# A Mamba-like block with an FFN on one core: the first step gets an order of its own, GpSimd splits W_in, TensorE transposes the identity while it waits, and the bias is prepared in two operations

## The chip, the cores and the metric

The kernel runs on one core of a Trainium2 chip. Its time is the device time of one execution in microseconds (us). Five engines take part, each with an instruction queue of its own, worked off in order: TensorE (PE), VectorE (DVE), ScalarE (ACT), GpSimd (POOL) and SyncE (SP), which here only issues transfers. They meet at semaphores alone: `then_inc` counts one up when an instruction is done, `wait_ge` holds a queue until it has reached a number.

## The reference, cut to what matters

```python
xn = layernorm(x)                                   # x: 4 x 1024 x 256
x_inner, z = split(xn @ W_in.T)                     # 512 channels each
xc = silu(causal_conv4(x_inner) + conv_b)
h[t] = 0.95 * h[t-1] + xc[t]                        # a scan over 1024 tokens
s_C = (xc @ W_x.T)[:, 16:]
y = (h * (s_C @ exp(B_log).T) * silu(z)) @ W_out.T
attn = layernorm(xn + y) * ln_g + ln_b
ffn = mx_quantise(xn) @ mx_quantise(W).T + bias     # blocks of 32, FP6 grid
out = x + attn + ffn
```

## The kernel before

A batch element is 1024 tokens. Per element the kernel holds the 512 channels as four chunks `c` of 128 partitions by 1024 tokens, and the tokens as two halves `g` of 512 (four tiles of 128). Every product in which precision matters is done as three fp32r matmuls on a high and a low part (`split_product`), so every operand is split first: ACT copies it to fp32r (`xn_high`, `y_high`, `w_in_high`), and DVE or POOL subtracts that from the original (`xn_low`, `y_low`, `w_in_low`).

The elements are pipelined by hand. `step(s)` of each engine lists, in the order of its queue, the work of three elements: `prev`, `here` and `nxt`. Functions wrapped in `of_batch` do nothing for an element that doesn't exist. `every_step` runs s = -1, 0, 1, 2, then `last_step` follows. Step -1 is thus only the front half of element 0 (`nxt`), with the preparation of the weights put between by `if first(nxt)`:

- DVE: token statistics, `scale_ffn_weight` and `round_ffn_weight` (L1208 to L1223, operations of 128x512 in SBUF), `w_in_low(0)`, `xn_low` of both halves, `dequantise_ffn_weight`, `block_max`, `w_in_low(1)`, the two middle taps of the convolution of chunks 0 and 1 (`conv_tap2`, `conv_tap1`, L1110), then `w_ffn_low`, `sum_w_out` and `scan` of chunk 0 (L1139).
- POOL: `rstd_1`, `prepare_b`, `prepare_bias`, `conv_tap0` of chunks 0 and 1 (L412), then `gate` of chunk 0 (L420).
- ACT: `normalise`, `w_in_high(0)`, `xn_high`, `w_in_high(1)`, `b_exponential`, `mask_b`, then `taps` of chunks 0 and 1, `silu_x(0)`.
- PE: `t_norm` of both halves (transposes of xn), `x_half` 0 to 2, `w_ffn_transposes` after `x_half(1)`, and `z_half`, `x_half(3)` and `s_product` when their PSUM slots come free.

`prepare_bias` makes two rows, high and low part of ln_b + ffn_b, for one matmul with ones; each of its seven POOL operations but the last waits in `chain` for its own end. It also scales g_row by 16, since `inverse_deviation` works on the sum of squares and not on the mean.

PSUM has three slots of two banks, which hold a chunk each, and two banks for the output. Which chunk lies in which slot stands in fixed lists, and `slot_free` makes PE wait for the last reader of what a slot held:

```python
SLOT_X = [1, 2, 0, 2]
SLOT_Z = [1, 1, 1, 2]
SLOT_TN = [0, 1]
SLOT_CB = [0, 1, 2, 0]
```

The loads of SP's queue are x of element 0 in two halves, W_in in two halves of columns (`w_in_f`, in the buffer rs), W_out, x of element 1, and, once that has landed, x of element 2. The small weights and the rows are loaded from ACT's queue.

## Time and profile before

| | |
|---|---|
| median of 3 runs | 264.28 us (263.95 to 264.28) |
| the profiled execution | 264.83 us, of it 263.0 us span from the first to the last instruction |
| DVE busy | 228.6 us, 87% of the span |
| PE busy | 216.9 us, 82% |
| POOL busy | 200.9 us, 76% |
| ACT busy | 154.6 us, 59% |
| mean granted clock of TensorE | 0.959 |

Busy time counts an instruction from its start to its end, and so holds the time in which one was started and stood still. The shares are of the whole span; the step that is changed takes about its first 35 us. In the rows below L12 is line 12 of the kernel, `out<-in` are tiles by name, and `<-` in brackets names what ended the idle time before.

### The profile page before, as it was taken

How to read it: one execution, taken by the hardware profiler on the slowest of the kernel's cores; microseconds unless marked ns; L12 is line 12 of the kernel's file. 1: busy time of each engine (PE TensorE's matmuls, PEld its weight loads, DVE VectorE, ACT ScalarE, POOL GpSimd, SP SyncE). 2: the span in 40 equal slices, each digit the busy share in tenths (PEclk: the TensorE clock that was granted, in tenths of full speed). 3: DMA queues.
4: the chain of work that ended last, by engine and by line, in shares of the span. 5: the costliest groups of instructions: out<-in, count | busy, mean ns of one | idle time of the engine just before them, and what ended most of it. 6: DMA issues, size and time to landing. Idle time of an engine off the chain costs nothing.

```text
span 263.0 us, 3473 instructions
## 1 busy us (share of the span) xinstructions
PE 216.9 (82%) x1252; PEld 180.8 (69%) x1252; DVE 228.6 (87%) x311; ACT 154.6 (59%) x234; POOL 200.9 (76%) x130
## 2 busy tenths in 40 slices
PE   0369974878899999879999969879999992977991
PEld 0348843357689886668898928767988951867991
DVE  3899999997799899958999999588999997594875
ACT  2796591455956537667995347728976364454320
POOL 1427949999997779999689599979498999933423
PEclk9999999797999999999999999979999998697999
DMA  7965000000000000004112000000202000002032
GB/s 230 262 217 159 1 2 0 0 1 0 0 2 0 1 2 0 0 2 150 40 53 80 0 0 1 2 0 0 82 0 80 4 0 0 0 2 80 26 137 80
DMA packets 10809, 11.18 MB, mean 42 GB/s; under 512 B 680, under 2 KB 10152, under 8 KB 10792
## 3 DMA queue, kind: packets, MB, share of 16 engines
q1 hardware_dynamic: 9520, 9.96, 11.8%
q10 hardware_dynamic: 1272, 0.99, 1.4%
q8 instruction: 10, 0.16, 0.3%
q14 instruction: 7, 0.06, 0.1%
HBM read 6.76 MB, written 4.19 MB: 42 GB/s over the span
## 4 chain that ended last, share of the span: by engine, by line
DVE 33%; POOL 27%; PE 16%; issue 10%; ACT 10%; DMA 4%; POOLq 0%; ACTq 0%; DVEq 0%
POOL hy L420 9%; POOL rstd L400 6%; DVE hy L1139 6%; POOL xc L412 6%; DVE xc L1110 6%; DVE fx L1177 3%; DVE rs L1167 2%; DMA y<-fx 2%; ACT xn L625 2%; DVE fx L1169 2%; DVE bn L1047 2%; DVE y_lo L1157 2%; DVE xq L1093 2%; ACT rs L718 2%; ACT y_hi L694 2%
## 5 line engine op out<-in xcount | busy, mean ns | idle before, releaser
L807 PE MATMUL slot<-xn_hi,w_in_lo 128*128 128x512 f32 x128 | 53.2, 416 | 6.1 <-DVE xn_lo L1099 2.6
L412 POOL TENSOR_TENSOR xc<-xc,tap 128x1021 f32<-128x1021 f32 x16 | 46.1, 2883 | 13.9 <-DVE xc L1110 13.9
L808 PE MATMUL slot<-xn_lo,w_in_hi 128*128 128x512 f32 x128 | 51.6, 403 | 0.0
L809 PE MATMUL slot<-xn_hi,w_in_hi 128*128 128x512 f32 x128 | 51.4, 402 | 0.0
L1139 DVE TENSOR_TENSOR_SCAN hy<-decay,xc 128x1024 f32<-128x1024 f32 x16 | 46.5, 2909 | 0.1
L420 POOL TENSOR_TENSOR hy<-hy,sz 128x1024 f32<-128x1024 f32 x14 | 43.4, 3098 | 2.3 <-ACT sz L672 2.3
L1110 DVE SCALAR_TENSOR_TENSOR xc<-slot,cw,xc 128x1023 f32<-128x1023 f32 (+1 forms) x32 | 40.2, 1265 | 2.1 <-ACT tap L662 1.6
L807 PEld LDWEIGHTS slot<-xn_hi,w_in_lo 128*128 128x128 f32 x128 | 24.7, 193 | 17.6 <-issue 3.9
L677 ACT ACTIVATE xc<-xc 128x1024 f32<-128x1024 f32 x16 | 17.0, 1060 | 29.0 <-POOL xc L412 29.0
L809 PEld LDWEIGHTS slot<-xn_hi,w_in_hi 128*128 128x128 f32 x128 | 24.7, 193 | 6.1
L808 PEld LDWEIGHTS slot<-xn_lo,w_in_hi 128*128 128x128 f32 x128 | 24.8, 193 | 4.9
L658 ACT ACTIVATE xc<-slot,cb,cw 128x1024 f32<-128x1024 f32 x16 | 19.2, 1201 | 12.7 <-PE slot L809 12.7
L625 ACT ACTIVATE xn<-x_in,nmr,rstd 128x256 f32<-128x256 f32 x32 | 16.6, 590 | 13.5 <-POOL nmr L404 13.3
L906 PE MATMUL obank<-w_out_hi,y_hi 128*128 128x256 f32 x96 | 24.3, 285 | 0.0
L905 PE MATMUL obank<-w_out_lo,y_hi 128*128 128x256 f32 x96 | 24.3, 285 | 0.0
L430 POOL TENSOR_TENSOR y_lo<-hy,y_hi 128x1024 fp32r<-128x1024 f32 x9 | 22.4, 2525 | 2.5 <-ACT y_hi L694 2.4
L803 PE MATMUL slot<-ident,xn 128*128 128x128 f32 x64 | 11.2, 332 | 14.5 <-ACT xn L625 11.7
L1152 DVE TENSOR_TENSOR hy<-slot,hy 128x1024 f32<-128x1024 f32 x16 | 18.9, 1210 | 3.3 <-PE slot L873 3.2
L400 POOL TENSOR_TENSOR rstd<-ve,minus_half 128x4 f32<-128x4 f32 x8 | 17.1, 2134 | 5.6 <-DVE ve L1063 5.6
L803 PEld LDWEIGHTS slot<-ident,xn 128*128 128x128 f32 x64 | 9.1, 172 | 16.4 <-issue 12.2
L872 PE MATMUL slot<-s_lo,b_t 128*128 128x512 f32 x32 | 14.7, 458 | 6.2 <-DVE s_lo L1145 5.9
L672 ACT ACTIVATE sz<-slot 128x1024 f32<-128x1024 f32 x14 | 14.3, 1024 | 7.7 <-POOL hy L420 7.4
(125 smaller groups left out, 586.3 us busy)
## 6 DMA issues: line engine op xcount, KB each, us to landing
x_in<-L_attn_x SPq DMA_DIRECT2D x3, 1024.0 KB, 5.4
y<-fx SPq DMA_DIRECT2D x6, 512.0 KB, 3.0
x_in<-L_attn_x SPq DMA_DIRECT2D x2, 512.0 KB, 4.1
rs<-L_attn_W_in SPq DMA_DIRECT2D x2, 512.0 KB, 10.0
y<-x_in SPq DMA_DIRECT2D x3, 256.0 KB, 2.1
fx<-L_attn_W_out SPq DMA_DIRECT2D x1, 512.0 KB, 12.9
fx<-L_ffn_weight ACTq DMA_DIRECT2D x1, 256.0 KB, 5.3
xc<-L_attn_B_log ACTq DMA_DIRECT2D x1, 256.0 KB
```

Of the source, the lines that this page charges most:

```text
L400: pool.tensor_tensor(rstd1[:, b % XS, cols], ve1[:, cols], minus_half[:, cols], ALU.pow).then_inc(rstd1_ready, 1)
L412: pool.tensor_tensor(xc[:, c, TAPS - 1:], xc[:, c, TAPS - 1:], tap0[:, c % 2, 0:n], ALU.add).then_inc(conv_ready, 1)
L420: pool.tensor_tensor(hy[:, c, :], hy[:, c, :], sz_of(b, c), ALU.mult).then_inc(hsz_ready, 1)
L430: pool.tensor_tensor(y_lo_of(b, c), hy[:, c, :], y_hi_of(b, c).bitcast(F32), ALU.subtract).then_inc(ylo_pool, 1)
L625: act.activation(xn[:, t, :], x_in[:, b % XS, t, :], ACT.Identity, bias=nmr1[:, b % XS, t:t + 1], scale=rstd1[:, b % XS, t:t + 1]).then_in ...
L807: pe.matmul(dst, w_lo, m_hi, start=first, stop=False)
L808: pe.matmul(dst, w_hi, m_lo, start=False, stop=False)
L809: return pe.matmul(dst, w_hi, m_hi, start=False, stop=last)
L905: pe.matmul(bank[:, 0:DM], y_hi[:, c, tok], w_out_lo[:, c, :], start=c == 0, stop=False)
L906: pe.matmul(bank[:, 0:DM], y_hi[:, c, tok], w_out_hi[:, c, :], start=False, stop=False)
L1110: dve.scalar_tensor_tensor(xc[:, c, back:], slot[SLOT_X[c]][:, 0:SEQ - back], cw[:, c, k:k + 1], xc[:, c, back:], ALU.mult, ALU.add).then_ ...
L1139: dve.tensor_tensor_scan(hy[:, c, :], decay[:, 0:1].broadcast_to([P, SEQ]), xc[:, c, :], 0.0, ALU.mult, ALU.add).then_inc(scan_done, 1)
```

## The change

- Step -1 becomes a function `first_step` of each engine, and `every_step` starts at 0. In it DVE does `block_max` right behind each `xn_low`; PE does `w_ffn_transposes` after `x_half(2)`; ACT does `b_exponential` and `mask_b` right behind `xn_high`, ahead of `taps`.
- Element 0 has PSUM slots of its own for x, z and the cb products, and the waits of PE follow them. `x_half(0)` waits for `xn_lo` half by half.
- `w_in_high` (ACT) and `w_in_low` (DVE) go; POOL does both in `split_w_in`, ahead of `prepare_b`.
- PE does 48 transposes of the identity ahead of `t_norm`, and 12 more ahead of `x_half(0)`.
- ln_b and ffn_b are loaded into two partitions each of a tile that POOL clears first; `prepare_bias` is one copy, and a subtraction over 64 partitions. The factor 16 of g_row goes, since `inverse_deviation` now divides by DM.
- SP waits for W_in before it issues the load of W_out.

```diff
+        FIRST_SLOT_X = [2, 0, 1, 0]
+        FIRST_SLOT_Z = [2, 1, 2, 1]
+        FIRST_SLOT_CB = [0, 2, 1, 0]
+        def slot_x(b, c):
+            return slot[(FIRST_SLOT_X if first(b) else SLOT_X)[c]]
...
-            for s in range(-1, LAST):
+            for s in range(LAST):
                 step(s)
...
+            sp.wait_ge(w_in_loaded[1], 16)
             sp.dma_start(w_out_f, w_out.rearrange("(c p) o -> p c o", p=P)).then_inc(w_out_loaded, 16)
...
+            pool.memset(bias_f, 0.0).then_inc(bias_cleared, 1)
             pool.memset(decay[:, :], DECAY).then_inc(const_ready, 1)
...
-                pool.tensor_scalar(ve2[:, cols], ssq[:, cols], DM * LN_EPS, None, ALU.add).then_inc(ve2_ready, 1)
+                pool.tensor_scalar(ve2[:, cols], ssq[:, cols], 1.0 / DM, LN_EPS, ALU.mult, ALU.add).then_inc(ve2_ready, 1)
...
+            def split_w_in(h):
+                cols = slice(h * DI, (h + 1) * DI)
+                pool.wait_ge(w_in_loaded[h], 16)
+                pool.tensor_copy(w_in_hi[:, :, cols], w_in_f[:, :, cols]).then_inc(w_in_hi_ready, 1)
+                pool.wait_ge(w_in_hi_ready, h + 1)
+                pool.tensor_tensor(w_in_lo[:, :, cols], w_in_f[:, :, cols], w_in_hi[:, :, cols].bitcast(F32),
+                                   ALU.subtract).then_inc(w_in_lo_ready, 1)
...
-                for i in range(3):
-                    pool.wait_ge(row_loaded[i], 16)
-                chain(pool.tensor_scalar(g_row[:, :], g_row[:, :], math.sqrt(DM), None, ALU.mult))
-                chain(pool.tensor_tensor(bias_a, bias_a, bias_b, ALU.add))
-                chain(pool.tensor_copy(bias_hi[:, :], bias_a))
-                chain(pool.tensor_tensor(bias_b, bias_a, bias_hi[:, :].bitcast(F32), ALU.subtract))
-                chain(pool.tensor_scalar(bias_b, bias_b, ident[:, 1:2], None, ALU.mult))
-                chain(pool.tensor_scalar(bias_a, bias_hi[:, :].bitcast(F32), ident[:, 0:1], None, ALU.mult))
-                pool.tensor_tensor(bias_rows[:, :], bias_a, bias_b, ALU.add).then_inc(bias_ready, 1)
+                pool.wait_ge(row_loaded[1], 16)
+                pool.wait_ge(row_loaded[2], 16)
+                chain(pool.tensor_copy(bias_rows[:, :], bias_f))
+                low = slice(P // 2, P)
+                pool.tensor_tensor(bias_rows[low, :], bias_f[low, :], bias_rows[low, :].bitcast(F32), ALU.subtract).then_inc(bias_ready, 1)
+                pool.wait_ge(bias_ready, 1)
+
+            def first_step(nxt):                       # POOL
+                rstd_1(nxt, 0)
+                rstd_1(nxt, 1)
+                split_w_in(0)
+                split_w_in(1)
+                prepare_b()
+                prepare_bias()
+                conv_tap0(nxt, 0)
+                conv_tap0(nxt, 1)
+                gate(nxt, 0)
...
-            for i, (dst, src) in enumerate(((g_row[:, :], ln_g), (bias_a, ln_b), (bias_b, ffn_b))):
-                act.dma_start(dst, src.rearrange("(a d) -> a d", a=1).broadcast_to([P, DM])).then_inc(row_loaded[i], 16)
+            act.dma_start(g_row[:, :], ln_g.rearrange("(a d) -> a d", a=1).broadcast_to([P, DM])).then_inc(row_loaded[0], 16)
+            act.wait_ge(bias_cleared, 1)
+            for i, src in enumerate((ln_b, ffn_b)):
+                act.dma_start(bias_f[i * P // 4:P:P // 2, :],
+                              src.rearrange("(a d) -> a d", a=1).broadcast_to([2, DM])).then_inc(row_loaded[1 + i], 16)
+
+            def first_step(nxt):                       # ACT
+                normalise(nxt, 0)
+                normalise(nxt, 1)
+                xn_high(nxt, 0)
+                xn_high(nxt, 1)
+                b_exponential()
+                mask_b()
+                taps(nxt, 0)
+                w_x_twice()
+                taps(nxt, 1)
+                w_ffn_high()
+                silu_x(nxt, 0)
+                taps(nxt, 2)
...
                 for g in range(2):
+                    if e0 == 0:
+                        pe.wait_ge(xn_lo_ready, 2 * b + g + 1)
...
+            def warm_up(n):
+                for i in range(n):
+                    transpose(obank[0][:, 0:P], ident[:, :])
+
+            def first_step(nxt):                       # PE
+                pe.wait_ge(ident_ready, 2)
+                warm_up(48)
+                t_norm(nxt, 0)
+                t_norm(nxt, 1)
+                warm_up(12)
+                x_half(nxt, 0)
+                x_half(nxt, 1)
+                x_half(nxt, 2)
+                w_ffn_transposes()
+                pe.wait_ge(tap1_done, 1)
+                z_half(nxt, 0)
+                pe.wait_ge(tap1_done, 2)
+                x_half(nxt, 3)
+                pe.wait_ge(tap1_done, 3)
+                z_half(nxt, 1)
+                pe.wait_ge(sz_ready, 1)
+                z_half(nxt, 2)
+                s_product(nxt)
+                pe.wait_ge(sz_ready, 2)
+                z_half(nxt, 3)
...
-                slot_free(nxt, (y_ready, NCH * here + 2, here))
+                slot_free(nxt, (y_ready, NCH * here + (3 if first(here) else 2), here))
                 t_norm(nxt, 1)
...
+            def first_step(nxt):                       # DVE
+                for g in range(2):
+                    token_stats(nxt, g)
+                    aggregate(nxt, g)
+                    mean_var(nxt, g)
+                scale_ffn_weight()
+                round_ffn_weight()
+                xn_low(nxt, 0)
+                block_max(nxt, 0)
+                xn_low(nxt, 1)
+                block_max(nxt, 1)
+                block_scale(nxt, 0)
+                dequantise_ffn_weight()
+                conv_tap2(nxt, 0)
+                conv_tap1(nxt, 0)
+                block_inverse(nxt, 0)
+                block_scale(nxt, 1)
+                conv_tap2(nxt, 1)
+                conv_tap1(nxt, 1)
+                w_ffn_low()
+                sum_w_out()
+                block_inverse(nxt, 1)
+                scan(nxt, 0)
```

## Rows read from the trace of the kernel before

**Rows 1.** The page: the span, and the chain that ended last, by engine.

```profile
span 263.0 us, 3473 instructions
...
DVE 33%; POOL 27%; PE 16%; issue 10%; ACT 10%; DMA 4%; POOLq 0%; ACTq 0%; DVEq 0%
```

**Rows 2.** Timeline of DVE, 9 to 36 us: start, duration (us), instruction, count, idle before.

```profile
10.26 0.43 DVE L1218 CAST hy<-fx 128x512 fp8e4<-128x512 f32 x1
10.72 0.69 DVE L1221 TENSOR_TENSOR fx<-hy,fx 128x512 f32<-128x512 fp8e4 x1
...
11.91 0.43 DVE L1223 TENSOR_SCALAR hy<-hy 128x512 f32<-128x512 f32 x1
13.45 1.22 DVE L1205 TENSOR_TENSOR w_in_lo<-rs,w_in_hi 128x1024 fp32r<-128x1024 f32 x1 [1.11 <-ACT w_in_hi L588]
14.60 2.35 DVE L1099 TENSOR_TENSOR xn_lo<-slot,xn_hi 128x1024 fp32r<-128x1024 f32 x2
...
18.30 1.66 DVE L1228 SCALAR_TENSOR_TENSOR fx<-fx,hy 128x512 f32<-128x512 f32 x1
...
24.98 2.60 DVE L1110 SCALAR_TENSOR_TENSOR xc<-slot,cw,xc 128x1023 f32<-128x1023 f32 x2 [0.30 <-ACT tap L662]
...
32.52 2.97 DVE L1139 TENSOR_TENSOR_SCAN hy<-decay,xc 128x1024 f32<-128x1024 f32 x1
35.41 0.72 DVE L1047 BATCH_NORM_STATS2 bn<-x_in 128x6 f32<-128x256 f32 x2
```

**Rows 3.** Timeline of POOL, first 34 us.

```profile
9.59 0.69 POOL L404 TENSOR_TENSOR nmr<-nm,rstd 128x4 f32<-128x4 f32 x1
...
17.75 1.67 POOL L484 TENSOR_TENSOR xc<-xc,b_t 128x512 f32<-128x512 f32 x1 [7.46 <-ACT b_t L594]
...
20.92 1.28 POOL L488 TENSOR_TENSOR b_t<-xc 128x512 fp32r<-128x512 f32 x1 [1.51 <-ACT xc L602]
...
29.40 3.94 POOL L412 TENSOR_TENSOR xc<-xc,tap 128x1021 f32<-128x1021 f32 x2
```

**Rows 4.** Timeline of ACT, 22 to 43 us.

```profile
22.62 1.21 ACT L658 ACTIVATE xc<-slot,cb,cw 128x1024 f32<-128x1024 f32 x1 [1.78 <-PE slot L809]
...
41.54 1.06 ACT L677 ACTIVATE xc<-xc 128x1024 f32<-128x1024 f32 x1 [1.87 <-POOL xc L412]
```

**Rows 5.** Timelines of DVE and POOL in the next steps: two pairs that overlap.

```profile
42.00 6.22 DVE L1139 TENSOR_TENSOR_SCAN hy<-decay,xc 128x1024 f32<-128x1024 f32 x2
...
71.22 0.70 DVE L1080 TENSOR_SCALAR s<-amax 128x32 f32<-128x32 f32 x1
...
42.02 4.05 POOL L412 TENSOR_TENSOR xc<-xc,tap 128x1021 f32<-128x1021 f32 x1 [0.51 <-DVE xc L1110]
...
71.85 5.75 POOL L430 TENSOR_TENSOR y_lo<-hy,y_hi 128x1024 fp32r<-128x1024 f32 x2
```

**Rows 6.** Groups of POOL by line and shape, 0 to 80 us: count, busy us, mean ns.

```profile
L500 POOL TENSOR_TENSOR w_out_lo<-fx,w_out_hi 128x1024 fp32r<-128x1024 f32 x1 | 2.4, 2384 | 0.0
...
L512 POOL CAST bias_hi<-hy 128x256 fp32r<-128x256 f32 x1 | 0.4, 397 | 0.1
...
L506 POOL CAST ones_r<-xc 128x128 fp32r<-128x128 f32 x1 | 0.3, 289 | 0.1
```

**Rows 7.** Busy time by stretch: length, PE, PEld, DVE, ACT, POOL, clock, DMA, GB/s.

```profile
17.00:22.60 5.60, 5.55 (x13) 4.43 (x14) 5.50 (x6) 3.46 (x6) 3.28 (x4) 1.00 0.45 137
...
63.00:63.50 0.50, 0.50 (x5) 0.50 (x4) 0.00 (x0) 0.50 (x1) 0.42 (x2) 0.50 0.00 0
64.00:64.50 0.50, 0.50 (x5) 0.41 (x4) 0.50 (x1) 0.00 (x0) 0.50 (x1) 1.00 0.00 0
```

**Rows 8.** Timeline of PE, 58 to 65 us: transposes.

```profile
60.64 1.94 PE L803 MATMUL slot<-ident,xn 128*128 128x128 f32 x8 [1.08 <-ACT xn L625]
```

**Rows 9.** The tile rs, into which W_in is loaded: issues and landings.

```profile
L353 SPq DMA_DIRECT2D rs<-L_attn_W_in x2: 469/484/500, 1.8 to 2.3; - x2
...
DMA to landing us min/median/max: 8.9/10.0/11.2
```

More of the change, by code:

```diff
@@ L293, in build, with slot_z, slot_cb @@
         SLOT_CB = [0, 1, 2, 0]
+        FIRST_SLOT_CB = [0, 2, 1, 0]
+        def slot_x(b, c):
+            return slot[(FIRST_SLOT_X if first(b) else SLOT_X)[c]]
+        def slot_z(b, c):
+            return slot[(FIRST_SLOT_Z if first(b) else SLOT_Z)[c]]
+        def slot_cb(b, c):
+            return slot[(FIRST_SLOT_CB if first(b) else SLOT_CB)[c]]
         def half(g):
@@ L468, in scale_g @@
                 wait(pool, norm_ready, NT * b + HT * (g + 1))
+                if first(b) and g == 0:
+                    pool.wait_ge(row_loaded[0], 16)
                 pool.tensor_tensor(rs[:, cols, :], rs[:, cols, :],
@@ L532, in step @@
                 dequantise(here, 1)
-                if first(nxt):
-                    prepare_b()
-                    prepare_bias()
                 y_low(here, 0)
@@ L671, in silu_z @@
                     wait(act, hsz_ready, NCH * b + c)
[L672 removed]
+                act.activation(sz_of(b, c), slot_z(b, c)[:, :], ACT.Silu).then_inc(sz_ready, 1)
             @of_batch
@@ L734, in step @@
                 normalise(nxt, 1)
-                if first(nxt):
-                    w_in_high(0)
                 norm_2(prev, 0)
@@ L839, in x_half @@
             def x_half(b, c):
-                if c == 0:
-                    wait(pe, xn_lo_ready, 2 * (b + 1))
-                    if first(b):
-                        pe.wait_ge(w_in_lo_ready, 1)
-                in_projection(SLOT_X[c], c * P, x_ready)
+                if c == 0 and first(b):
+                    pe.wait_ge(w_in_lo_ready, 1)
+                in_projection(b, slot_x(b, c), c * P, x_ready)
             @of_batch
@@ L871, in cb_product @@
                 for g in range(2):
-                    pe.matmul(slot[SLOT_CB[c]][:, half(g)], b_t[:, c * P:(c + 1) * P], s_lo[:, half(g)], start=True, stop=False)
-                    mm = pe.matmul(slot[SLOT_CB[c]][:, half(g)], b_t[:, c * P:(c + 1) * P], s_hi[:, half(g)],
+                    pe.matmul(slot_cb(b, c)[:, half(g)], b_t[:, c * P:(c + 1) * P], s_lo[:, half(g)], start=True, stop=False)
+                    mm = pe.matmul(slot_cb(b, c)[:, half(g)], b_t[:, c * P:(c + 1) * P], s_hi[:, half(g)],
                                    start=False, stop=True)
@@ L976, in step @@
                 x_half(nxt, 1)
-                if first(nxt):
-                    w_ffn_transposes()
                 slot_free(nxt, (xd_lo_ready, 2 * here + 2, here), (xn_lo_ready, 2 * nxt + 1, nxt))
@@ L1268, in step @@
                 y_product(here, 2)
-                if first(nxt):
-                    scale_ffn_weight()
-                    round_ffn_weight()
-                    w_in_low(0)
                 xn_low(nxt, 0)
@@ L1276, in step @@
                 xn_low(nxt, 1)
-                if first(nxt):
-                    dequantise_ffn_weight()
                 block_max(nxt, 0)
@@ L1288, in step @@
                 block_inverse(nxt, 0)
-                if first(nxt):
-                    w_in_low(1)
                 conv_tap2(nxt, 0)
@@ L1296, in step @@
                 conv_tap1(nxt, 1)
-                if first(nxt):
-                    w_ffn_low()
-                    sum_w_out()
                 block_inverse(nxt, 1)
```

41 lines of the change are left out of this document (12 added, 29 removed).

## The prediction

> **What bounds the kernel now.** I read the page first, then the timelines of the first 60 us, engine by engine. By the chain of work that ended last, no single engine sets the end: DVE has 33% of it and POOL 27% [rows 1]. So what the changed step gives is read at one place, the end of DVE's first scan, behind which DVE and POOL run without a break into step 0. It is started at 32.52 and DVE's next instruction comes at 35.41 [rows 2]. A scan needs only 2.1 us (below), so it really began at 33.3. That is the end of POOL's two `conv_tap0`, 29.40 + 3.94 [rows 3]. Three queues arrive there together: DVE, in order, at 32.5; POOL, late because `prepare_b` and `prepare_bias` hold it until 29.4; ACT and PE, which give `taps(0)` at 22.62, when `x_half(0)` is done [rows 4].
>
> **A resource that both DVE and POOL need.** At 42.0 us DVE has two scans in 6.22 us, and POOL started a `conv_tap0` at 42.02 that took 4.05, where two at 29.40 took 3.94 together, 1.97 each [rows 3, 5]. One after the other fits: scan 2.1, tap 2.0, scan 2.1, sum 6.2. And the instruction that waited goes ahead of a successor of the one that ran. The same holds for a plain TENSOR_SCALAR: DVE's of 128x32 at 71.22 took 0.70, while one of 128x512 takes 0.43, and it ended at 71.92, just after the POOL operation before the one of 71.85 had ended [rows 2, 5]. In the changed step itself: L1228 took 1.66, where L1221 of the same width took 0.69, while POOL's L484 ran to 19.42, and that took 1.67 against 1.28 for L488 [rows 2, 3]. So DVE's instructions that work from SBUF alone and POOL's exclude each other for a whole instruction. `xn_low` is not among these: it reads PSUM and keeps its 1.2 us [rows 2].
>
> The Trainium skill (SBUF — State Buffer, Who interferes with whom) says the same: an exclusive lock, held for a whole instruction, against DVE instructions with two SBUF inputs or in a two-port mode, while `tensor_reduce` and those with one SBUF input are free. The durations above agree. By a plain reading of the change without this rule, the sum would be that of the first rival.
>
> **The change, part by part.**
>
> *GpSimd splits W_in.* It takes 1.22 us twice and 1.11 us of idle from DVE [rows 2], and two copies from ACT, and puts four operations on POOL. The subtractions are like L500: 2.38 us each. The copies have no row at 128x1024: by the casts, 0.289 us at 128 columns and 0.397 at 256, it is 0.108 per 128, so 0.397 + 6 x 0.108 = 1.05 us [rows 6]. The lower bound is 1.0; the upper one is that of a two-input operation, 2.38 [rows 6]. I take 1.05, the same operation being nearest. All four: 6.9 us.
>
> When do they start? POOL is free at 10.28 [rows 3]; the first half of W_in lands at 1.8 + 8.9 = 10.7 [rows 9], perhaps a little earlier since W_out no longer shares the queue. There DVE is in `round_ffn_weight`: L1218 until 10.69, L1221 from 10.72 [rows 2]. Two orders are possible.
>
> Order A, the copy comes first: copy 10.7 to 11.7, L1221 to 12.4, subtraction to 14.8, L1222 to 15.2, second copy to 16.3, L1223 to 16.7, second subtraction to 19.1. DVE's rounding ends at 16.7, not 12.3, and `xn_low(0)` begins at 16.7 instead of 14.60 [rows 2]: 2.1 later.
>
> Order B, L1221 comes first: L1221 to 11.4, copy to 12.5, L1222 to 12.9, subtraction to 15.3, L1223 to 15.7, then the second pair to 19.2. `xn_low(0)` begins at 15.7.
>
> *DVE's queue from there.* Before, it was 24.98 - 14.60 = 10.4 us from `xn_low(0)` to `conv_tap2(0)` [rows 2]. Of this go `w_in_low(1)` 1.2, idle 0.30, and the 1.0 that L1228 stood still; a reciprocal of 0.3 moves behind. That leaves 7.6. POOL's `prepare_b` is later now: its first operation 19.15 to 20.4 (1.28) meets only `xn_low` and `block_max`; the mask on ACT takes 1.5 as before (from 19.42 to 20.92) [rows 3]; its second, from 21.9, and the two casts of 0.29 and 0.40 fall among the four operations of `dequantise_ffn_weight`, each before one of them: 1.28 + 0.29 + 0.40 = 2.0. In order A `conv_tap2(0)` begins at 16.7 + 7.6 + 2.0 = 26.3, in order B at 25.2 (some 0.1 less standing still), against 24.98. From it to the scan were 7.54 us [rows 2]; the order within is the same. The scan begins at 33.8 in A and 32.7 in B, and now at once, since POOL, with the short bias, ends `conv_tap0(1)` by then. It ends at 35.9 in A (+0.5), at 34.8 in B (-0.6).
>
> *ACT and PE.* `taps(0)` now stands behind the mask: 21.9 - 0.1 = 21.8, 0.8 earlier than 22.62 [rows 4]. Its data reach DVE 2.36 later, at 24.2, before DVE is free. `x_half(0)` waits for `xn_lo` (17.9 and 20.1 in A) and takes 12 matmuls; it is ready by 21.6 at full clock, 23.2 at the half. Both are covered by DVE's 26.3. So the warm-up and the half-by-half wait are worth nothing here, and 1.6 us if that cover is gone. The clock: 13 matmuls took 5.60 us at the start, 0.43 each, which is the 1.2 GHz level for 512 columns, though the granted-clock column has 1.00 there [rows 7]. Do transposes lift it? At 60.64 eight took 1.94 us; only transposes ran from there to 63.5, still at 0.50, and at 64.0 the clock was 1.00 [rows 7, 8]. I take it that they do. If the clock stayed at half throughout, 48 transposes some 0.22 us apart (1.94 less the tail of the last, over seven) would run from 1.5 to 12.0, `t_norm` to 15.6, twelve more to 18.2 and `x_half(0)` to 23.4: DVE would have its taps at 25.8, still before 26.3.
>
> The Trainium skill (TensorE: Matmul & The Clock Gate, Part 4: PE-mode transpose) speaks against this: in transpose mode the full clock doesn't engage. The rows at 64 us disagree. By the page the two warm-ups are a delay, which the third rival prices.
>
> *The bias.* Seven POOL operations and their waits between 22.2 and 29.4 [rows 3] become a copy (0.40) and a subtraction (0.7, as half of L488's 1.28 for twice the width). That takes 7.2 - 1.1 = 6.1 us off POOL, where the split puts 6.9 on. Without it the scan would end some 5 us later; with it POOL is ready for `conv_tap0(0)` at 27.0, before its data at 28.8.
>
> *PSUM slots.* `z_half(1)` now waits for DVE's taps of chunk 2, which were done a `conv_tap0` before 41.54, so 39.5, and in A 40.0 [rows 4]; with 2.8 us for it and 1.0 for `silu_z(1)` that is 43.9, so `silu_x(2)` ends at 45.0 instead of 42.6 [rows 4]. The second scan at 42.0 needs it, but begins only after the POOL tap between, at 46.1 [rows 5], 46.6 in A. Hidden, with 1.6 us to spare. `t_norm(1, 1)` waits for one more y product, which ends about when its xn does: 0.1.
>
> *The rest.* A memset of 128x256 on POOL, some 0.3 us, delays ACT's loads; W_out and x of element 1 are issued some 10 us later (behind 2.3 + 11.2 = 13.5 [rows 9]), and are wanted from 30 us on: nothing. From 36 us the two queues are as before.
>
> The sum: A +0.5, B -0.6. The landing time can't be told from L1221's start to 0.1 us, so I take the middle, 0.0: 264.8 against the profiled 264.83 (263.0 span and 1.8 around it). That execution lies 0.55 above the median of 264.28, so I predict 264.2.
>
> **Rivals.**
>
> *First, faster: the exclusion hardly bites, or falls elsewhere.* Then POOL's split is done at 17.7, the mask at 20.5, `taps(0)` at 20.5, `conv_tap2(0)` at 22.9, and the next at 25.9 instead of 27.9. The scan runs from 30.6 to 32.7: 35.41 - 32.7 = -2.7, 262.1 profiled, 261.6 as median. For it: PE and ACT would be early enough, with the clock lifted. Against it: rows 5. Half of it, if some of the five collisions fall away. 0.28.
>
> *Second, slower: the copy on POOL is dear.* At 2.38 us each, the split ends at 21.8, `b_t` begins at 24.6 and pushes `dequantise`, `conv_tap2(0)` begins at 28.9, the scan ends at 38.7: +3.3, 268.1 profiled. It decides from about 1.3 us a copy, where two times 0.25 and the stalls add 0.6. Speaks for it: nothing wide of the kind is in the trace; against it, the two casts. 0.14.
>
> *Third, the first rival without the clock.* If transposes don't lift it, 48 x 0.22 end at 12, `t_norm` at 15.6, 12 more at 18.2, `x_half(0)` at 23.4: `taps(0)` 0.8 later than before, and the gain of the first rival is gone, about +0.1. That also is the case in which the change doesn't do what it says. 0.10.
>
> *The main case*, the exclusion takes back what is gained, 0.48, from -0.8 to +1.0 profiled.
>
> **How the numbers follow.** What a measurement of this kernel can tell from no change is 0.2%, 0.53 us. The main case lies faster than that with 0.12, within with 0.26, slower with 0.10. Faster: 0.28 + 0.12 = 0.40. Same: 0.26 + 0.06 of the third = 0.32. Slower: 0.14 + 0.10 + 0.04 = 0.28. The range: the main case's own is 263.5 to 265.3; down to 262.2 it takes in the most of the first rival but its last 0.6 us, up to 266.0 half of the second. Left out are about 0.08 and 0.10.
>
> **What would show it.** L1221 to L1223 two to three times as long as before, each ending with a POOL operation of `split_w_in`; copies of 1.05 us; `xn_low(0)` starting at 15.7 to 16.7; `taps(0)` right behind the mask, near 21.8; DVE without idle ahead of `conv_tap2(0)`; matmuls of `x_half(0)` 0.23 us apart or 0.43; the scan taking 2.1 us, not 2.97. The prediction is wrong if DVE waits for ACT's taps there, if W_in lands after 11.4 (then the stalls shift behind the rounding), or if the shift at 36 us isn't kept to the end, because DVE and POOL meet in another order in later steps.

## The result: slower by 1.4%, and the profile after

The changed kernel takes 268.15 us (266.83 to 269.64, 4 runs) against 264.18 (263.95 to 264.28, 4 runs) for the kernel before: a ratio of 1.0139, 95% interval 1.0091 to 1.0186. I had forecast 264.2 with a range up to 266.0. The profiled execution took 268.78 us.

The page of the changed kernel: the span, busy time by engine, the chain that ended last by engine, and the load of the FFN weight with its median time from issue to landing.

```profile
span 266.9 us, 3591 instructions
...
PE 225.6 (85%) x1312; PEld 189.8 (71%) x1312; DVE 228.8 (86%) x309; ACT 152.7 (57%) x232; POOL 201.6 (76%) x130
...
DVE 37%; POOL 20%; PE 19%; issue 9%; ACT 7%; DMA 6%; POOLq 0%; ACTq 0%; DVEq 0%
...
fx<-L_ffn_weight ACTq DMA_DIRECT2D x1, 256.0 KB, 9.3
```

DVE's busy time is what it was, 228.8 against 228.6, with two subtractions of 1.22 us fewer: the time in which started instructions stand still ("held", below) has filled their place. POOL has fallen from 27% to 20% of the chain, and DMA risen from 4 to 6 [rows 1].

The timeline of DVE, after, 11 to 54 us; it answers to [rows 2]:

```profile
11.17 0.69 DVE L1262 TENSOR_REDUCE hy<-fx 128x16 f32<-128x512 f32 x1 [2.74 <-DMA fx<-L_ffn_weight]
11.89 1.44 DVE L1263 TENSOR_SCALAR hy<-hy 128x16 f32<-128x16 f32 x1
...
13.66 1.18 DVE L1266 TENSOR_TENSOR fx<-fx,hy 128x512 f32<-128x512 f32 x1
14.87 2.45 DVE L1269 CAST hy<-fx 128x512 fp8e4<-128x512 f32 x1
17.35 1.63 DVE L1272 TENSOR_TENSOR fx<-hy,fx 128x512 f32<-128x512 fp8e4 x1
...
19.95 1.23 DVE L1156 TENSOR_TENSOR xn_lo<-slot,xn_hi 128x1024 fp32r<-128x1024 f32 x1
...
29.26 2.60 DVE L1167 SCALAR_TENSOR_TENSOR xc<-slot,cw,xc 128x1023 f32<-128x1023 f32 x2 [1.84 <-ACT tap L689]
...
36.55 2.32 DVE L1196 TENSOR_TENSOR_SCAN hy<-decay,xc 128x1024 f32<-128x1024 f32 x1
38.80 1.37 DVE L1104 BATCH_NORM_STATS2 bn<-x_in 128x6 f32<-128x256 f32 x4
...
50.09 3.86 DVE L1196 TENSOR_TENSOR_SCAN hy<-decay,xc 128x1024 f32<-128x1024 f32 x1 [2.42 <-ACT xc L704]
53.87 1.38 DVE L1104 BATCH_NORM_STATS2 bn<-x_in 128x6 f32<-128x256 f32 x4
```

And that of POOL, after; it answers to [rows 3]:

```profile
1.44 0.31 POOL L401 MEMSET hy<- 128x256 f32 x1
...
9.82 1.04 POOL L506 CAST w_in_hi<-rs 128x1024 fp32r<-128x1024 f32 x1
10.94 2.36 POOL L508 TENSOR_TENSOR w_in_lo<-rs,w_in_hi 128x1024 fp32r<-128x1024 f32 x1
13.24 1.04 POOL L506 CAST w_in_hi<-rs 128x1024 fp32r<-128x1024 f32 x1
14.37 2.67 POOL L508 TENSOR_TENSOR w_in_lo<-rs,w_in_hi 128x1024 fp32r<-128x1024 f32 x1
...
45.41 4.05 POOL L423 TENSOR_TENSOR xc<-xc,tap 128x1021 f32<-128x1021 f32 x1 [0.51 <-DVE xc L1167]
49.42 2.38 POOL L431 TENSOR_TENSOR hy<-hy,sz 128x1024 f32<-128x1024 f32 x1
```

Read the two together. The same cast that took DVE 0.43 us (L1218 in [rows 2]) takes 2.45 and ends at 17.32; POOL's second subtraction runs from 14.37 to 17.04. L1263, on 16 columns, takes 1.44 and ends at 13.33, when POOL's first subtraction ends (13.30). Four of DVE's operations are held so, by 1.27, 0.49, 2.02 and 0.94 us over what they take where POOL does not split (0.17, 0.69, 0.43, 0.69): 4.7 in all. The last of them, L1272, lies beside the first operation of `prepare_b` (17.00 to 18.44), which follows the split at once. Ahead of them stands an idle 2.74, for a weight that lands late. `xn_low(0)` begins at 19.95, not 14.60; the first scan ends at 38.80, not 35.41 (+3.4 us). The next time DVE comes to token statistics is at 53.87, against 48.14 before (+5.7), behind a scan that waited 2.42 us for ACT, and then ran past POOL's `gate` of 49.42 (to 51.80) and took 3.86. The span ended 3.9 us later.

TensorE, after, at the start, when x and z of element 0 begin, and once in between:

```profile
1.51 7.91 PE L834 MATMUL obank<-ident 128*128 128x128 f32 x48 [1.51 <-POOL ident L398]
...
12.12 1.06 PE L834 MATMUL slot<-ident,xn 128*128 128x128 f32 x8 [0.90 <-ACT xn L652]
...
21.32 0.77 PE L838 MATMUL slot<-xn_hi,w_in_lo 128*128 128x512 f32 x1 [6.82 <-DVE xn_lo L1156]
21.88 0.63 PE L839 MATMUL slot<-xn_lo,w_in_hi 128*128 128x512 f32 x1
...
27.27 0.39 PE L840 MATMUL slot<-xn_hi,w_in_hi 128*128 128x512 f32 x1
...
42.87 0.79 PE L838 MATMUL slot<-xn_hi,w_in_lo 128*128 128x512 f32 x1 [4.28 <-DVE xc L1167]
```

Busy time by stretch of the changed kernel (columns as in [rows 7]):

```profile
14.00:17.00 3.00, 0.50 (x5) 0.26 (x3) 2.96 (x2) 2.89 (x5) 2.92 (x3) 0.97 0.95 322
17.00:20.00 3.00, 0.00 (x0) 0.00 (x0) 2.86 (x5) 1.33 (x2) 1.49 (x3) 0.50 0.57 188
20.00:23.00 3.00, 1.68 (x4) 1.43 (x5) 3.00 (x3) 0.00 (x0) 2.73 (x5) 0.50 0.66 176
```

The warm-up had lifted the clock: the eight transposes of xn at 12.12 take 1.06 us, where the same eight take 1.94 in e7 below, without a warm-up. (The granted clock doesn't tell it: it reads 0.97 at 14 to 17 us here, and 1.00 there in e3 and e7, without a warm-up.) Then TensorE stood idle for 6.82 us until `xn_lo` was there, the granted clock fell to 0.50, and `x_half(0)` ran with 0.43 us from matmul to matmul, the 1.2 GHz level; from 27.27 on it is 0.23. ACT and then DVE waited for it (1.84 us).

### The profile page after: what moved, and what is told of

The parts are those of the page before. It is cut to its first block, busy times and chain, and to the rows that moved or that the text cites. A ratio compares the mean times of both kernels' runs of the same rounds, so it can differ in the third digit from the quotient of the medians.

```text
span 266.9 us, 3591 instructions
## 1 busy us (share of the span) xinstructions
PE 225.6 (85%) x1312; PEld 189.8 (71%) x1312; DVE 228.8 (86%) x309; ACT 152.7 (57%) x232; POOL 201.6 (76%) x130
## 4 chain that ended last, share of the span: by engine, by line
DVE 37%; POOL 20%; PE 19%; issue 9%; ACT 7%; DMA 6%; POOLq 0%; ACTq 0%; DVEq 0%
DVE xc L1167 8%; POOL hy L431 8%; DVE hy L1196 6%; POOL rstd L411 6%; POOL xc L423 5%; DMA fx<-L_ffn_weight 3%; DVE fx L1234 2%; DVE rs L1224 2%; DMA y<-fx 2%; DVE fx L1226 2%; PE slot L838 2%; PE slot L840 2%; PE slot L839 2%; DVE xq L1150 2%; DVE y_lo L1214 2%
## 5 line engine op out<-in xcount | busy, mean ns | idle before, releaser
L838 PE MATMUL slot<-xn_hi,w_in_lo 128*128 128x512 f32 x128 | 54.0, 422 | 11.8 <-DVE xn_lo L1156 7.2
L839 PE MATMUL slot<-xn_lo,w_in_hi 128*128 128x512 f32 x128 | 52.3, 408 | 0.0
L840 PE MATMUL slot<-xn_hi,w_in_hi 128*128 128x512 f32 x128 | 52.1, 407 | 0.0
L1196 DVE TENSOR_TENSOR_SCAN hy<-decay,xc 128x1024 f32<-128x1024 f32 x16 | 44.8, 2799 | 2.4 <-ACT xc L704 2.4
L431 POOL TENSOR_TENSOR hy<-hy,sz 128x1024 f32<-128x1024 f32 x14 | 41.3, 2948 | 2.2 <-DVE hy L1196 2.2
L838 PEld LDWEIGHTS slot<-xn_hi,w_in_lo 128*128 128x128 f32 x128 | 25.3, 198 | 23.1 <-issue 11.2
L903 PE MATMUL slot<-s_lo,b_t 128*128 128x512 f32 x32 | 15.9, 496 | 10.5 <-DVE s_lo L1202 10.5
L699 ACT ACTIVATE sz<-slot 128x1024 f32<-128x1024 f32 x14 | 14.3, 1023 | 10.7 <-PE slot L840 6.4
L460 POOL TENSOR_SCALAR ve<-ssq 128x4 f32<-128x4 f32 (+2 forms) x11 | 3.8, 347 | 19.5 <-ACT sq_out L731 10.0
L937 PEld LDWEIGHTS obank<-w_out_hi,y_hi 128*128 128x128 f32 x96 | 18.3, 191 | 0.0
```

The source lines that it names most:

```text
L431: pool.tensor_tensor(hy[:, c, :], hy[:, c, :], sz_of(b, c), ALU.mult).then_inc(hsz_ready, 1)
L838: pe.matmul(dst, w_lo, m_hi, start=first, stop=False)
L839: pe.matmul(dst, w_hi, m_lo, start=False, stop=False)
L840: return pe.matmul(dst, w_hi, m_hi, start=False, stop=last)
L937: pe.matmul(bank[:, 0:DM], y_hi[:, c, tok], w_out_hi[:, c, :], start=False, stop=False)
L1196: dve.tensor_tensor_scan(hy[:, c, :], decay[:, 0:1].broadcast_to([P, SEQ]), xc[:, c, :], 0.0, ALU.mult, ALU.add).then_inc(scan_done, 1)
```

## The experiments

The theory after the result: the split on POOL holds DVE's rounding of the FFN weight, and the memset of `bias_f` delays the weight's load. The rivals: TensorE's clock and its idle time are the loss; the new PSUM slots are it; or the new order on DVE and ACT. Each run has a ratio to the kernel before, timed on the same chip (medians of before: 264.63, 264.56 and 264.53 us for e1 to e4, e5 to e8 and e9 to e12). As a second measure the table has three starts of DVE's token statistics from the traces: behind the first scan (of element 1, first half), the second half of the same, and element 3's.

| kernel | median us (range, runs) | ratio (95%) | first | second | third |
|---|---|---|---|---|---|
| before | 264.18 (263.95 to 264.28, 4) | | 35.41 | 48.14 | 142.04 |
| after | 268.15 (266.83 to 269.64, 4) | 1.0139 (1.0091 to 1.0186) | 38.80 | 53.87 | 147.47 |
| e1 memset late | 266.37 (264.62 to 268.22, 9) | 1.0078 (1.0034 to 1.0122) | 38.14 | 53.22 | 146.87 |
| e2 split on ACT and DVE | 264.60 (263.83 to 267.69, 10) | 1.0014 (0.9978 to 1.0051) | 35.89 | 48.71 | 143.60 |
| e3 no warm-up | 269.16 (267.04 to 269.52, 4) | 1.0157 (1.0097 to 1.0217) | 39.74 | 54.82 | 148.65 |
| e4 old slots | 271.01 (269.74 to 272.37, 4) | 1.0261 (1.0201 to 1.0321) | 40.52 | 53.25 | 146.93 |
| e5 = e1, rounding later | 264.49 (263.35 to 266.40, 10) | 1.0010 (0.9973 to 1.0047) | 34.77 | 49.84 | 143.72 |
| e6 = e1 + e2 | 263.81 (262.42 to 264.27, 10) | 0.9976 (0.9945 to 1.0006) | 33.79 | 48.87 | 142.49 |
| e7 = e6, no warm-up | 264.13 (261.88 to 264.97, 10) | 0.9984 (0.9950 to 1.0019) | 33.89 | 48.98 | 142.64 |
| e8 before + a memset | 266.02 (263.75 to 267.37, 10) | 1.0054 (1.0015 to 1.0093) | 36.35 | 49.08 | 142.94 |
| e9 = after, z slots | 268.33 (267.58 to 270.92, 4) | 1.0156 (1.0102 to 1.0210) | 39.78 | 52.51 | 146.24 |
| e10 = e6, z slots | 262.66 (261.36 to 263.82, 11) | 0.9928 (0.9898 to 0.9958) | 33.98 | 46.70 | 140.50 |
| e11 = e5, z slots | 263.23 (261.66 to 264.28, 12) | 0.9947 (0.9916 to 0.9978) | 34.74 | 47.47 | 141.24 |
| e12 before + short bias | 262.75 (261.30 to 263.86, 11) | 0.9927 (0.9898 to 0.9956) | 33.71 | 46.44 | 140.21 |

### e1: the memset behind the one of `decay`

```diff
-            pool.memset(bias_f, 0.0).then_inc(bias_cleared, 1)
             pool.memset(decay[:, :], DECAY).then_inc(const_ready, 1)
+            pool.memset(bias_f, 0.0).then_inc(bias_cleared, 1)
```

> The changed kernel with one line moved: the memset of the bias tile stands behind that of decay, so ACT issues its loads 0.25 us earlier, ahead of SP's load of W_in. Theory 1 (the late landing of the FFN weight, 11.15 us against 6.9, starves DVE and shifts its rounding into GpSimd's split): the weight lands near 7 us again, DVE's first operation on it starts near 8.3, xn_low(0) near 16.7 instead of 19.95, and the time falls by about 3 us from the changed kernel's 268.15. Rival (the landing is a matter of the bandwidth shared, not of the order of issue): it still lands near 11 us and the time stays within 0.5 us of the changed kernel.

The weight is issued at 1.58 us again and is there at 8.58. Yet the first scan ends only 0.66 earlier, since DVE now comes to its rounding earlier and meets all of POOL's split. Timelines of DVE and POOL in e1:

```profile
9.79 1.56 DVE L1266 TENSOR_TENSOR fx<-fx,hy 128x512 f32<-128x512 f32 x1
11.39 2.48 DVE L1269 CAST hy<-fx 128x512 fp8e4<-128x512 f32 x1
13.90 1.40 DVE L1272 TENSOR_TENSOR fx<-hy,fx 128x512 f32<-128x512 fp8e4 x1
15.34 2.45 DVE L1273 TENSOR_SCALAR hy<-fx 128x512 uint32<-128x512 uint32 x1
17.82 1.37 DVE L1274 TENSOR_SCALAR hy<-hy 128x512 f32<-128x512 f32 x1
19.22 1.23 DVE L1156 TENSOR_TENSOR xn_lo<-slot,xn_hi 128x1024 fp32r<-128x1024 f32 x1
```

```profile
9.77 1.04 POOL L506 CAST w_in_hi<-rs 128x1024 fp32r<-128x1024 f32 x1
...
14.84 2.66 POOL L508 TENSOR_TENSOR w_in_lo<-rs,w_in_hi 128x1024 fp32r<-128x1024 f32 x1
17.47 1.44 POOL L497 TENSOR_TENSOR xc<-xc,b_t 128x512 f32<-128x512 f32 x1
```

Five operations take 9.26 us; in e6, where ACT and DVE split, they take 0.69 + 0.43 + 0.69 + 0.43 + 0.43 = 2.67. The 6.6 us between come one operation for one: four of DVE's beside the four of the split, which POOL has from 9.77 to 17.50, and the fifth beside the first of `prepare_b`. The first four are held for 5.65 us, where the split takes 1.04 + 2.36 + 1.04 + 2.4 = 6.8 by itself; the fifth for 0.94.

### e2: the split back on ACT and DVE, everything else as after

```diff
@@ POOL, first_step
-                split_w_in(0)
-                split_w_in(1)
@@ ACT, first_step
+                w_in_high(0)
                 xn_high(nxt, 0)
                 xn_high(nxt, 1)
+                w_in_high(1)
@@ DVE, first_step
                 round_ffn_weight()
+                w_in_low(0)
...
                 dequantise_ffn_weight()
+                w_in_low(1)
```

> The changed kernel with the split of W_in back on ACT and DVE, at the places that it had. Theory 1 (the weight is late, and GpSimd's split blocks DVE on top, 4.5 us of standing still in the rounding): with the split gone from GpSimd the rounding takes 4.0 us from 11.17 and ends near 15.2, xn_low(0) starts near 16.4 and the first scan ends near 35, 3.8 earlier; time about 264.5 to 265.5. Rival (the blocking is harmless, the clock and the late weight make the loss): the scan ends at 38 to 39 and the time stays near 268.

The first scan ends 2.9 us earlier than after, though the weight is later still:

```profile
12.02 0.69 DVE L1273 TENSOR_REDUCE hy<-fx 128x16 f32<-128x512 f32 x1 [3.57 <-DMA fx<-L_ffn_weight]
...
46.50 2.29 DVE L1201 TENSOR_TENSOR_SCAN hy<-decay,xc 128x1024 f32<-128x1024 f32 x1 [1.74 <-ACT xc L707]
```

So the split is the larger part of the loss, though DVE has two subtractions more to do here. From the first mark to the second this kernel takes 12.82 us and not 15.07, though z lies in the new slots; the part on the prediction comes back to that.

### e3: no warm-up

```diff
@@ PE, first_step
-                warm_up(48)
@@
-                warm_up(12)
```

> The changed kernel without its 60 transposes of the identity. Theory 1 (TensorE has waited 6.8 us when x_half(0) starts and the clock has fallen by then, so the transposes buy nothing): the same time as the changed kernel within 0.5 us, x_half(0) at 0.43 us a matmul in both. Rival (they give back something, or cost something by the phase in which the clock rises later): a difference of 1 us or more, on either side.

Inconclusive by its time: 0.9 us later at the first mark, in an execution in which the weight landed 0.8 later (11.97) and the first half of W_in late too, so that POOL began to split at 10.91 instead of 9.82. `x_half(0)` has 0.43 us from matmul to matmul in both kernels: the idle 6.82 us undoes the warm-up. e7 asks the question again.

### e4: the PSUM slots as before

```diff
-        FIRST_SLOT_X = [2, 0, 1, 0]
-        FIRST_SLOT_Z = [2, 1, 2, 1]
+        FIRST_SLOT_X = [1, 2, 0, 2]
+        FIRST_SLOT_Z = [1, 1, 1, 2]
...
                 warm_up(12)
+                pe.wait_ge(xn_lo_ready, 2)
                 x_half(nxt, 0)
```

(the cb slots and the waits of z, `s_product` and `t_norm(1, 1)` with them)

> The changed kernel with the PSUM slots and the PE waits of the first element as they were. Theory 1 (z_half(1) waits 4.3 us for the taps of chunk 2, runs at the lower clock and makes silu_z(1), silu_x(2) and the third scan late: DVE is idle 2.4 us and the stretch from the first scan's end to the second token_stats takes 15.1 us instead of 12.7): that stretch falls to about 12.7 and the time by 1 to 2.4 us. Rival (the step is set by DVE and GpSimd blocking each other anyway, and what is lost there is won back in the next step): within 0.5 us of the changed kernel.

The x slots and the z slots pull against each other. With the old ones `x_half(0)` waits for both `xn_lo`, the first scan ends 1.7 us later; but from the first mark to the second it is 12.73 us, as before, and not 15.07. I had expected 1 to 2.4 us less than the changed kernel. The median is 2.9 above it, although the third mark comes 0.5 earlier (146.93 against 147.47); where the rest is lost no run shows.

### e5: e1, with the rounding behind `block_max`

```diff
                 scale_ffn_weight()
-                round_ffn_weight()
                 xn_low(nxt, 0)
                 block_max(nxt, 0)
                 xn_low(nxt, 1)
                 block_max(nxt, 1)
+                round_ffn_weight()
```

> The changed kernel with the memset of the bias tile behind that of decay, and DVE's round_ffn_weight behind the second block_max instead of ahead of xn_low: while GpSimd splits W_in, DVE has only xn_low and block_max, which don't exclude it. Theory 1 (the exclusion is the loss): xn_low(0) starts at once behind ACT's xn_high, near 13.0 instead of 19.2, x_half(0) near 14.2 to 15, the subtractions on GpSimd take 2.4 us each, DVE's queue up to conv_tap2(0) ends near 24 to 25, the first scan ends by 34, and the time is 261 to 263.5, under the kernel before. Rival (the exclusion only moves into dequantise and the mask, and DVE's work in order is what counts): the scan ends near 36 and the time is that of the kernel before or above, 264 to 266.

POOL splits as in e1, but DVE now spends that time in work that reads PSUM or reduces. Timeline of DVE in e5:

```profile
13.31 1.23 DVE L1156 TENSOR_TENSOR xn_lo<-slot,xn_hi 128x1024 fp32r<-128x1024 f32 x1 [3.19 <-ACT xn_hi L660]
14.45 1.21 DVE L1129 TENSOR_REDUCE amax<-xn 128x32 f32<-128x1024 f32 x1
...
17.83 1.38 DVE L1269 CAST hy<-fx 128x512 fp8e4<-128x512 f32 x1
...
20.90 1.29 DVE L1137 TENSOR_SCALAR s<-amax 128x32 f32<-128x32 f32 x1
...
45.50 4.42 DVE L1196 TENSOR_TENSOR_SCAN hy<-decay,xc 128x1024 f32<-128x1024 f32 x1 [1.86 <-ACT xc L704]
```

and of POOL:

```profile
41.38 4.05 POOL L423 TENSOR_TENSOR xc<-xc,tap 128x1021 f32<-128x1021 f32 x1 [0.51 <-DVE xc L1167]
```

`xn_low` and `block_max` keep 1.2 us beside POOL; the first scan ends 3.4 us earlier than in e1, with not one operation added or taken away. That is the cleanest test of the exclusion. (The loads did not land alike: in e5 the weight came 2.0 us earlier and let DVE start on it at 8.22 instead of 8.58, and W_in about 1 us later. `xn_low(0)` at 13.31 hangs on neither, it waits for ACT.) The time, 264.49, is that of the kernel before, not under it as I had expected. The Trainium skill (SBUF — State Buffer, Who interferes with whom) lists `tensor_reduce` and instructions with one SBUF input as free of GpSimd's lock, and those with two SBUF inputs or in a two-port mode as bound by it: here it agrees, with 1.21 and 1.23 us against 1.40 for 0.69 and 2.45 for 0.43 in e1.

### e6: both, the late memset and the split on ACT and DVE

> The changed kernel with the split of W_in back on ACT and DVE, and the memset of the bias tile behind that of decay. The late weight cost DVE some 3 us of idle time in the run with the split back alone (idle 3.57 ahead of the first operation on it, at 12.02). Theory 1 (that is a loss of its own): DVE starts on the weight near 8.5, is through the rounding near 12.5, xn_low(0) near 14.2 instead of 17.2, and the time falls by 2 to 3 us to about 262. Rival (TensorE and ACT come late anyway): the scan moves by less than 1 us and the time stays at 264 to 265.

```profile
45.04 3.90 DVE L1201 TENSOR_TENSOR_SCAN hy<-decay,xc 128x1024 f32<-128x1024 f32 x1 [2.38 <-ACT xc L707]
```

With e1, e2 and after this makes a square at the first mark: 38.80 with both causes, 38.14 with the split alone, 35.89 with the early memset alone, 33.79 with neither. Alone the split costs 4.35 us and the memset 2.1; together 5.0, since a DVE that waits for the weight cannot be held by POOL. In medians the pair costs 268.15 - 263.81 = 4.3 us; the split alone (e1 against e6) only 2.6, the profiled execution of e1 being the slowest of its runs, and the memset alone (e2 against e6) 0.8. The early part is now 1.6 us ahead of the kernel before, and the median is not: from the first mark to the second it still takes 15.08 us, and a scan waits 2.38.

### e7: e6 without the warm-up

(both calls of `warm_up` removed, as in e3)

> The kernel of the run before this one (split on ACT and DVE, memset late) without the 60 transposes of the identity. Here TensorE may stand on the path. Theory 1 (the warm-up is worth something only when x_half(0) follows it at once): x_half(0) starts near 15.5, at 0.43 us a matmul without and 0.23 with the transposes, taps(0) comes 2 us later without, and the time is 1 to 2 us longer than with them. Rival (DVE covers it): within 0.5 us of the run with them.

The second and third matmul of `x_half(0)` in e6, which began at 15.88:

```profile
16.19 0.40 PE L844 MATMUL slot<-xn_lo,w_in_hi 128*128 128x512 f32 x1
16.43 0.39 PE L845 MATMUL slot<-xn_hi,w_in_hi 128*128 128x512 f32 x1
```

and, in e7, the eight transposes of `t_norm` ahead of it and its first three:

```profile
12.51 1.94 PE L839 MATMUL slot<-ident,xn 128*128 128x128 f32 x8 [0.46 <-ACT xn L655]
...
15.93 0.76 PE L843 MATMUL slot<-xn_hi,w_in_lo 128*128 128x512 f32 x1 [1.48 <-DVE xn_lo L1159]
16.49 0.63 PE L844 MATMUL slot<-xn_lo,w_in_hi 128*128 128x512 f32 x1
16.92 0.63 PE L845 MATMUL slot<-xn_hi,w_in_hi 128*128 128x512 f32 x1
```

Here the warm-up does what it can: 0.24 us from matmul to matmul instead of 0.43. It is the twelve transposes right ahead of `x_half(0)` that do it: after an idle 1.34 us the eight before them took 1.94 us in e6 too. It is worth 0.1 us at the first mark, and the medians' intervals overlap: the rival holds, DVE covers it.

### e8: the kernel before with one memset

```diff
+            pool.memset(tap0[:, 0, 0:DM], 0.0)
             pool.memset(decay[:, :], DECAY).then_inc(const_ready, 1)
```

> The kernel before with one operation more: a memset of 128x256 on GpSimd ahead of that of decay, which delays ACT's first load by 0.25 us, to behind SP's load of W_in. It adds no other work. Theory 1 (the order of issue sets when the FFN weight lands): it lands near 11 us instead of 6.9, DVE is idle some 3 us, xn_low(0) and the first scan move by 2.5 to 3.5 us, and the time rises to about 266 to 267. Rival (the landing has another cause, the wait of SP or the shorter bias loads): it lands near 7 us and the time is that of the kernel before, within 0.5 us.

All that is added is a memset of 0.3 us at 1.4 us, in a buffer that nothing has yet written. The weight is issued at 1.84 instead of 1.58:

```profile
11.27 0.69 DVE L1212 TENSOR_REDUCE hy<-fx 128x16 f32<-128x512 f32 x1 [2.88 <-DMA fx<-L_ffn_weight]
```

That costs the kernel before 0.94 us at the first mark, where I had expected 2.5 to 3.5, and 0.54% of its time. `xn_low(0)` begins 1.86 us later (16.46); of this the kernel before takes back about 1.1, since DVE then no longer waits for ACT's taps and its scan no longer for POOL (2.25 us instead of 2.89).

### e9, e10, e11: z on slots that don't wait for a tap

```diff
-        FIRST_SLOT_Z = [2, 1, 2, 1]
+        FIRST_SLOT_Z = [2, 2, 2, 1]
...
-                pe.wait_ge(tap1_done, 3)
-                z_half(nxt, 1)
                 pe.wait_ge(sz_ready, 1)
+                z_half(nxt, 1)
+                pe.wait_ge(sz_ready, 2)
                 z_half(nxt, 2)
                 s_product(nxt)
-                pe.wait_ge(sz_ready, 2)
+                pe.wait_ge(tap1_done, 3)
                 z_half(nxt, 3)
```

> The changed kernel with z_half(1) and z_half(2) of the first element in slot 2, behind silu_z(0) and silu_z(1) as in the kernel before, and z_half(3) behind the taps of chunk 2; x_half(0) keeps its early slot. Theory 1 (the new place of z_half(1) costs 2.3 us in step 0, whatever comes ahead of it): the first scan's end stays near 38.8, the stretch from there to the second token_stats falls from 15.1 to 12.7 us, and the time from 268.15 to about 266. Rival (the run with all the old slots had that stretch and was not faster, since the time is won back later): the stretch falls and the time stays within 0.7 us of the changed kernel.

> Split of W_in on ACT and DVE, memset late (the fourth of the run before), and z_half(1) and z_half(2) as in the kernel before. Theory 1: the first scan ends near 33.8 as there, 1.6 us earlier than in the kernel before, the next stretch takes 12.7 us, and the time is 1.5 to 2.5 us under the kernel before, near 262.5. Rival (what is won by 50 us is lost where DVE and GpSimd meet in another order): within 0.7 us of the kernel before.

> The changed kernel with the split on GpSimd, memset late, the rounding of the FFN weight behind block_max, and z_half(1) and z_half(2) as in the kernel before. Theory 1: the first scan ends near 34.8 as with the rounding later alone, the next stretch takes 12.7 instead of 15.1 us, and the time is 0.5 to 1.5 us under the kernel before. Rival: as for the run before this one, no difference that can be measured.

From the first mark to the second all three need 12.72 to 12.73 us instead of 15.07. DVE in e10:

```profile
40.56 6.22 DVE L1201 TENSOR_TENSOR_SCAN hy<-decay,xc 128x1024 f32<-128x1024 f32 x2
```

How much of the 2.35 us stays, traces and medians tell differently: from the first mark to the third it is 108.7 us in e6 and 106.5 in e10, and the profiled spans are 261.9 and 259.5; the medians differ by 1.15 us between e6 and e10, and by 1.26 between e5 and e11. On the changed kernel itself (e9) four runs show no gain; in its profile the weight landed at 11.49, POOL waited 1.44 us for W_in and began to split at 11.04 instead of 9.82, and the first mark came 1.0 us later, so that it neither speaks for the slots nor against them.

### e12: the kernel before with the short bias alone

(`prepare_bias`, the loads of the rows and the factor 16 as in the change, the memset behind the one of `decay`; order, slots, split and transposes as before)

> The kernel before with the short bias preparation alone (four bias rows loaded into a cleared tile, one copy and one subtraction, no factor on g_row); its memset stands behind that of decay. Theory 1 (in the kernel before GpSimd's taps, late by the bias, held the first scan from 32.5 to 33.3): conv_tap0(0) starts at the end of DVE's taps, near 27.5, the scan takes 2.3 us instead of 2.97 and ends near 34.7, and the time falls by 0.5 to 0.9 us. Rival (the two collide elsewhere then): no difference.

POOL in e12:

```profile
27.12 2.00 POOL L413 TENSOR_TENSOR xc<-xc,tap 128x1021 f32<-128x1021 f32 x1 [3.74 <-DVE xc L1115]
```

POOL now waits 3.74 us for DVE, where it came to `conv_tap0` 2 us late before [rows 3]. The first scan ends 1.70 us earlier, the third mark is 1.83 us earlier, and the median is 1.8 lower: of all edits this is the only one that gains, and the whole of it stays. That is more than the 0.5 to 0.9 us that I had expected. Of the 1.70, 0.65 are the scan, which no longer waits for POOL, and 0.46 lie between `conv_tap2(0)` and the scan. But 0.50 are there ahead of the bias, for `xn_low(0)` starts at 14.10 and not 14.60: POOL's L404 of [rows 3], held to 0.69 us there by a DVE operation on the weight, takes 0.20 in this execution, in which the weight landed 1.7 us later. That part is no doing of the edit, so how the median comes to 1.8 is shown only in part.

## Why the prediction was wrong

By medians the change comes apart so: before to e12, the short bias, -1.8 us; e12 to e10, the new order on DVE and ACT, the x slots, the warm-up, the wait of W_out and the half-by-half wait together, -0.1, that is nothing; e10 to e6, the z slots, +1.15; e6 to after, the split on POOL and the memset's place, +4.3. The sum is +3.6 over the 264.53 that the kernel before took beside e12; the 3.97 measured are over its 264.18 beside the changed kernel. The runs of the changed kernel spread over 2.8 us. Two of the signs that the prediction had named for being wrong are there: DVE waits for ACT's taps (1.84 us), and the shift at 36 us isn't kept. The steps below are in the order of time; the second and the fourth cost the most.

**The mechanism, right.** That DVE's work from SBUF and POOL's exclude each other, that this falls on the rounding of the weight, and that `xn_low` stays free, are shown by e1, e2 and e5. So is the way in which the two queues take turns, one operation for one, that orders A and B were worked out with. The prices of single operations held: copy 1.04 us (1.05 forecast), subtraction 2.36 (2.38). The second rival falls with them.

**The step that failed first: "A memset of 128x256 on POOL, some 0.3 us, delays ACT's loads", put down as nothing.** The memset did take 0.31 us. But ACT's queue waited with it, and its load of the weight came behind SP's of W_in (1.83 against 1.76 us, where it had been 1.58). It landed at 11.15 instead of 6.9, past the point where DVE wants it. That the memset does it is shown on either side, by e8 and e1. By itself it cost 2.1 us at the first mark (e2 against e6), with the split in place 0.66 (e1). The reason that I gave, that they are wanted from 30 us on, was one for W_out and x alone.

**The second: order A, "`xn_low(0)` begins at 16.7 instead of 14.60".** It began at 19.95, and at 19.22 with the weight in time. The sum had three operations of DVE behind three of the split, which holds them for 4.4 us (the rounding ends at 16.7, not 12.3); 2.1 is what is left of that when `w_in_low(0)` and its wait have gone. Held were 6.6 us in e1. The turns are those of the sum, but where they begin is not: of W_in's first half I had said that it lands at 10.7; in e1 it was there when POOL began at 9.77, and DVE, 0.25 us later than in the kernel before, stood at L1266. So all four operations of the split fell beside the rounding and not three, and the first of `prepare_b`, which follows at once, beside a fifth. Where the weight is late it is no better: `xn_low(0)` begins 10.1 us behind the start of the split in the changed kernel, e3, e4 and e9 alike (9.82, 10.91, 9.72 and 11.04), though the weight landed between 10.7 and 12.0. For such a pair of queues the term to take is the length of all that the other engine does in one go, 8.1 us here (the split's 6.8 and 1.28 for the first of `prepare_b`), of which 6.6 came; a landing that varies by a microsecond can't carry a sum that depends on the order of two instructions.

**The third: "Both are covered by DVE's 26.3".** The warm-up was "worth nothing here, and 1.6 us if that cover is gone". The cover was the 2.0 us for which `prepare_b` and the casts were to hold DVE in `dequantise_ffn_weight`. These collisions did not come: POOL was through at 22.88, DVE came there at 24.55, and from `xn_low(0)` it was ready for `conv_tap2(0)` after 7.46 us (27.41), not 9.6. `x_half(0)` starts from the same `xn_low(0)`; TensorE had stood idle for 6.82 us, the clock had fallen behind the warm-up, the twelve matmuls ran at 0.43 us each, and DVE waited 1.84 us for the taps. At 0.23 us each they would have been 2.4 us shorter, by my estimate, and DVE would not have waited. From the forecast's 35.9 to 38.80: +3.25 for `xn_low(0)`, -0.3 up to `conv_tap2(0)` (9.31 us instead of 9.6), -0.25 from there to the scan (7.29 against 7.54), +0.15 for the scan (2.25, not 2.1), together +2.85.

**The fourth: the slots, "Hidden, with 1.6 us to spare".** The start of `z_half(1)` was right, 4.1 us behind the first mark (42.87 in the changed kernel, 37.87 in e6; forecast 40.0 behind 35.9). The term that failed is "2.8 us for it": TensorE had stood idle for 4.28 us, so the clock was at the half, and ACT's `silu_z(1)` came 5.2 us later, at 48.08. That is 2.4 more, against 1.6 to spare, and `silu_x(2)` was done at 50.05. POOL's tap had ended at 49.46; DVE's scan, which should have stood ready there, came 0.6 late, found POOL in its `gate` (49.42 + 2.38 = 51.80), and ended at 53.95. So the half clock made the scan 0.6 late, and the turn that it missed cost the 2.35 us. Two more traces show that it is the turn and not the lateness. In e5 the scan was ready at 45.50, 0.07 us behind the end of the tap (45.43), and the stretch took 15.07 us all the same. In e2, with the same slots and a scan ready at 46.50, just ahead of the tap's end at 46.55, it took 12.82.

**The bias: "Without it the scan would end some 5 us later".** Argued with the split in place, which no run took apart. POOL, with it, was through at 22.88 and not at 27.0. Alone it gains 1.8.

**The clock, right with no effect.** Forty-eight transposes took 7.91 us, and e6 shows what follows them at 0.24 us a matmul, against 0.43 in e7: transposes lift it. The Trainium skill (TensorE: Matmul & The Clock Gate, Part 4: PE-mode transpose) says that the full clock doesn't engage in transpose mode; these runs don't bear that out. The third rival falls. The first, that the exclusion hardly bites, falls with e1.

What stays open: why medians show less than traces, 2.6 us against 4.35 for e1 and e6, and 1.15 against 2.0 at the third mark for e6 and e10. Of e1, e3 and e5 the profiled execution is the slowest of its runs. Of e4, e8, e10 and e12 it is the fastest. The turn of the second stretch hangs on a tenth of a microsecond (e2, e5), so other executions of e6 may catch it; no run shows how many do. Nor is the shift kept exactly: 3.39 us at the first mark was 5.73 at the second, 5.43 at the third and 3.9 at the end. I did not follow it through the later steps.
